# Banded attention with a side network: layer norm shared between GpSimd and VectorE, first transposes row by row, value weights split first, bias additions moved to step 0, output weights of the last pair kept

## Chip, cores and metric

One core of one Trainium2 chip runs the kernel alone. The metric is the device time in microseconds (us), the median over the runs of one kernel. A profile of one further execution goes with it. TensorE (PE) multiplies and transposes, ScalarE (ACT) and VectorE (DVE) work between PSUM and SBUF, GpSimd (POOL) works in SBUF, and all transfers are issued from the queue of SyncE (SP).

## The reference

```
xn  = layernorm(x)                         # x: 8 x 1024 x 512, over the last axis
Q,K,V = xn @ Wq + bq, xn @ Wk + bk, xn @ Wv + bv     # 16 heads of 64
S   = Q K^T where |i-j| <= 64, and 0 elsewhere        # masked scores stay in the softmax as zeros
out = x + (softmax(S) V) @ Wo + bo
        + (sum_h relu(s * W1 + b1) W2 + b2) @ Wout + bout,   s = xn @ Win + bin    # 64 wide, 16 inner
```

All inputs and outputs are float32.

## The kernel before

The batch has 8 items, and the 16 heads are 8 pairs. Every pair of an item is one step, numbered n = 8b + k (b the item, k the pair). There are 64 such steps and two more that drain the pipeline. Step n projects pair k of item b (`proj`), attends to the pair of step n-1 (`attend`) and multiplies the pair of step n-2 with its slice of Wo (`out_proj`). The order of the work on each engine is written out by hand, one function `step` for each engine, and engines wait for each other by counting semaphores. Instructions of one engine start in program order.

Matrix operands are split into a high and a low float32r part, and each product is three passes: high by high, high by low, low by high. The high part is a ScalarE copy, the low part a subtraction: on VectorE where the source is in PSUM, on GpSimd for weights (`split_low`, L328), for the attention output (`output_low`, L364) and for the output weights (L396). A projection (`project`, L1021) is 12 matmuls of 512 columns.

In item 0 (steps 0 to 7) the raw weights of a pair are loaded and split one step ahead, and the split form is also written to DRAM (`w_kept`, `wo_kept`). From item 1 on the split form is loaded from there. The output weights of pair 7 are the exception: `wo_kept` gets pairs 0 to 6 only, and pair 7's are loaded raw and split again in every item, at the end of its k = 0 step (ScalarE L662, then GpSimd L396), and also in step 64 for the last item.

Layer norm: VectorE takes the statistics (L681, L701) and aggregates them (L688). GpSimd then computes four small results: variance plus epsilon (L313), its power -1/2 (L315), mean times that (L318) and the negated shift (L323). ScalarE writes the normalised rows xn (`normalise`, L422), TensorE transposes them (`transpose_x`, L986), ScalarE and VectorE split the transposes (`x_high` L428, `x_low` L695). For item 0 this stands ahead of step 0, in two halves of four row tiles. For item b+1 the statistics are spread over steps k = 3 to 5 of item b, and the four small operations run on GpSimd in step k = 5. There they stand ahead of GpSimd's weight subtractions `split_low(n+1, V)` and `split_low(n+1, Q)` (item 0 only) and of both `output_low`:

```
if attend:
    normalise_weights(1)
if k == 5 and not last:
    layer_norm(b + 1, slice(0, T), b + 3, 4 * b + 8)
if split_next:
    split_low(n + 1, V_)
    split_low(n + 1, Q_)
```

The bias rows bo + bout are added to the accumulator on GpSimd (`add_biases`, L371): four row tiles in step k = 0, two in step k = 1 between the two `normalise_weights`, and two more in step k = 1 between `output_low(0)` and `output_low(1)`.

Other names used below: `mask_scores` (DVE L733, then L739 for the negated row maximum), `exps` (ACT L449), `denominators` (DVE L744, L747, L749), `normalise_weights` (POOL L358), `weigh_values` (PE L1088), `project_out` (PE L1038), `add_output` (DVE L756), `network_out` and `add_network` (PE L1060, DVE L786), `value_lines` (ACT L477).

## Time and profile before

| | us |
|---|---|
| median of 3 runs | 2365.82 (2365.38 to 2368.52) |
| the profiled execution | 2367.19 |
| its span in the trace | 2365.4 |
| PE busy | 2310.1 (98%) |
| DVE busy | 1960.6 (83%) |
| ACT busy | 1576.8 (67%) |
| POOL busy | 892.6 (38%) |

The span is the time from the first to the last instruction in the trace; 1.8 us of the execution lie around it. PE's busy share counts matmuls, whose ends are modelled. The mean granted TensorE clock is 0.996 of 2.4 GHz.

### The profile page before, as it was taken

The numbers are of one execution on the slowest core, as the hardware profiler recorded it, in microseconds if no ns is written. First come the engines' busy times: TensorE is split into PE (matmuls) and PEld (weight loads), VectorE is DVE, ScalarE is ACT, GpSimd is POOL, SyncE is SP. The second block draws the span as 40 slices with busy tenths as digits, with TensorE's granted clock in tenths as the row PEclk, the third lists the DMA queues.
The fourth block names the chain that finished last, engine by engine and source line by source line (L and its number), as shares of the span: only waits on it lengthen the run. The fifth ranks groups of instructions, "written<-read, shape, count | busy, mean of one in ns | idle before, by whom it ended". The sixth has DMA issues, their size and how long they took to land.

```text
span 2365.4 us, 43885 instructions
## 1 busy us (share of the span) xinstructions
PE 2310.1 (98%) x14913; PEld 1975.8 (84%) x14913; DVE 1960.6 (83%) x5088; ACT 1576.8 (67%) x4289; POOL 892.6 (38%) x1302
## 2 busy tenths in 40 slices
PE   5999999999999999999999999999999999999996
PEld 4787888888888888888888888888888888888885
DVE  4887779887898878988889878898879888798886
ACT  3776667666676667666667666766676666676664
POOL 3544435333343324334243332443334332443332
PEclk9999999999999999999999999999999999999999
DMA  4231213221132121421223221331212311122211
GB/s 136 86 125 55 103 59 108 72 72 59 46 123 75 54 75 34 138 65 54 66 63 109 71 57 56 91 98 54 77 46 90 107 55 59 54 89 64 66 47 45
DMA packets 69501, 177.58 MB, mean 75 GB/s; under 512 B 6536, under 2 KB 18848, under 8 KB 69280
## 3 DMA queue, kind: packets, MB, share of 16 engines
q1 hardware_dynamic: 69280, 174.78, 23.6%
q8 instruction: 121, 1.98, 0.3%
q14 instruction: 100, 0.82, 0.1%
HBM read 141.73 MB, written 33.03 MB: 74 GB/s over the span
## 4 chain that ended last, share of the span: by engine, by line
PE 93%; DVE 3%; issue 2%; ACT 1%; POOL 1%; DMA 0%; POOLq 0%; SPq 0%; ACTq 0%; DVEq 0%
PE ps L1021 43%; PE ps L1038 15%; PE ps L1088 12%; PE ps L1076 9%; PE ps L1009 7%; PE ps L1066 2%; PE ps L986 1%; PE ps L1048 1%; DVE probs L733 1%; PE ps L1060 1%; DVE xn L773 1%; DVE v_back L973 0%; ACT probs L449 0%; DVE o_sum L810 0%; DMA acc<-in_L_attn_x 0%
## 5 line engine op out<-in xcount | busy, mean ns | idle before, releaser
L1021 PE MATMUL ps<-xT_hi,w_split 128*128 128x512 f32 x3072 | 1040.7, 400 | 8.1 <-POOL w_split L328 5.0
L358 POOL TENSOR_SCALAR probs<-probs,inv_l,neg_e 128x256 f32<-128x256 f32 x1024 | 569.2, 577 | 638.1 <-DVE neg_e L749 638.1
L1021 PEld LDWEIGHTS ps<-xT_hi,w_split 128*128 128x128 f32 x3072 | 578.4, 188 | 135.3 <-issue 5.2
L449 ACT ACTIVATE probs<-probs,neg_max 128x256 f32<-128x256 f32 x1024 | 507.0, 498 | 142.0 <-DVE neg_max L739 140.9
L1021 PE MATMUL ps<-xT_lo,w_split 128*128 128x512 f32 x1536 | 600.4, 391 | 0.0
L756 DVE TENSOR_TENSOR acc<-ps,acc 128x512 f32<-128x512 f32 x512 | 344.4, 685 | 164.1 <-PE ps L1038 162.6
L500 ACT ACTIVATE pT_hi<-ps 128x512 fp32r<-128x512 f32 x512 | 278.1, 599 | 225.7 <-PE ps L1088 139.5
L364 POOL TENSOR_TENSOR oT_lo<-o_sum,oT_hi 128x512 fp32r<-128x512 f32 x128 | 163.7, 1294 | 682.9 <-ACT oT_hi L516 681.9
L733 DVE CUSTOM_DVE_ANT_0 probs<-ps,mask 128x256 f32<-128x256 f32 x1024 | 372.6, 419 | 31.7 <-PE ps L1009 31.3
L800 DVE TENSOR_TENSOR pT_lo<-ps,pT_hi 128x512 fp32r<-128x512 f32 x512 | 328.2, 684 | 51.1 <-ACT pT_hi L500 50.6
L1038 PE MATMUL ps<-wo_split,oT_hi 128*128 128x512 f32 x1024 | 331.2, 405 | 12.4 <-POOL wo_split L396 5.2
L1021 PEld LDWEIGHTS ps<-xT_lo,w_split 128*128 128x128 f32 x1536 | 290.2, 189 | 51.9
L1088 PE MATMUL ps<-pT_lo,v 128*128 128x256 f32 (+1 forms) x1280 | 306.3, 280 | 0.0
L1088 PE MATMUL ps<-pT_hi,v 128*128 128x256 f32 (+1 forms) x1280 | 302.6, 275 | 0.5 <-DVE pT_lo L800 0.5
L1076 PE MATMUL ps<-ident,probs 128*128 128x128 f32 x2048 | 258.3, 273 | 4.9 <-POOL probs L358 4.0
L1076 PEld LDWEIGHTS ps<-ident,probs 128*128 128x128 f32 x2048 | 230.4, 140 | 23.3 <-issue 3.0
L1088 PEld LDWEIGHTS ps<-pT_lo,v 128*128 128x128 f32 x1280 | 244.1, 191 | 5.1
L1088 PEld LDWEIGHTS ps<-pT_hi,v 128*128 128x128 f32 x1280 | 243.1, 190 | 5.9 <-DVE pT_lo L800 0.8
L1038 PEld LDWEIGHTS ps<-wo_split,oT_hi 128*128 128x128 f32 x1024 | 182.8, 190 | 51.9 <-issue 10.2
L1038 PE MATMUL ps<-wo_split,oT_lo 128*128 128x512 f32 x512 | 201.9, 394 | 0.0
L810 DVE SCALAR_TENSOR_TENSOR o_sum<-ps,v_back,o_part 64x512 f32<-64x512 f32 x256 | 190.8, 745 | 12.9 <-ACT o_part L509 9.0
L449 ACT ACTIVATION_READ_ACCUMULATOR probs<-probs,neg_max 128x1 f32 x1024 | 192.9, 188 | 0.0
(92 smaller groups left out, 3125.1 us busy)
## 6 DMA issues: line engine op xcount, KB each, us to landing
w_split<-w_kept SPq DMA_DIRECT2D x168, 512.0 KB, 3.6
wo_split<-wo_kept SPq DMA_DIRECT2D x49, 512.0 KB, 4.4
out_x<-acc SPq DMA_DIRECT2D x16, 1024.0 KB, 5.9
acc<-in_L_attn_x SPq DMA_DIRECT2D x15, 1024.0 KB, 7.7
w_kept<-w_split SPq DMA_DIRECT2D x24, 512.0 KB, 5.5
wo_raw<-in_L_attn_Wo SPq DMA_DIRECT2D x15, 256.0 KB, 4.8
wo_kept<-wo_split SPq DMA_DIRECT2D x7, 512.0 KB, 3.0
w_raw<-in_L_attn_Wv SPq DMA_DIRECT2D x8, 256.0 KB, 5.5
```

The costliest lines, as they stand in the source:

```text
L358: pool.tensor_scalar(probs[:, h, t], probs[:, h, t], inv_l[:, c:c + 1], neg_e[:, c:c + 1], ALU.mult, ALU.add).then_inc(normed, 1)
L449: act.activation(probs[:, h, t], probs[:, h, t], ACT.Exp, bias=neg_max[:, c:c + 1], accum_out=row_sum[:, c:c + 1])
L500: act.activation(pT[u % 2][hi][:, c * LINE:c * LINE + LINE], ps[PT_BANK[u][c]][:], ACT.Copy) \
L733: dve.tensor_tensor_reduce(out=probs[:, h, t], in0=ps[SCORE_BANK[tp][h]][:, i * WIN:i * WIN + WIN], in1=mask[:], scale=1.0, scalar=0.0, op ...
L756: dve.tensor_tensor(acc[:, parity, t], ps[OUT_BANK[t]][:], acc[:, parity, t], ALU.add) \
L800: dve.tensor_tensor(pT[u % 2][lo][:, cols], ps[PT_BANK[u][c]][:], f32(pT[u % 2][hi][:, cols]), ALU.subtract).then_inc(pT_lo, 1)
L810: dve.scalar_tensor_tensor(o_sum[half][rows], ps[PV_BANK[u]][rows], v_back[rows], o_part[h][rows], ALU.add, ALU.add).then_inc(o_summed, 1)
L1009: last = pe.matmul(ps[SCORE_BANK[tp][h]][:, i * WIN:i * WIN + WIN], qT[qp][rows, t * P:t * P + P], kT[kp][rows, t * P:t * P + WIN], start= ...
L1021: last = pe.matmul(dst[:], w[wp][:, i, c], xT[xp][:, c, half * LINE:half * LINE + LINE], start=(c == 0 and a == 0), stop=(c == KC - 1 and ...
L1038: last = pe.matmul(ps[OUT_BANK[t]][:], oT[op][:, t * P:t * P + P], wo[wp][:], start=(a == 0), stop=(a == 2))
L1076: last = pe.transpose(ps[PT_BANK[u][c]][:, i % 4 * P:i % 4 * P + P], probs[:, h, t, i % 2 * P:i % 2 * P + P], ident[:])
L1088: last = pe.matmul(ps[PV_BANK[u]][:, q0:q0 + (end - first) * P], v[:, (4 * half + c) % T, h].rearrange("p a d -> p (a d)"), pT[h][part][:, ...
```

## The change

- Layer norm. VectorE now adds epsilon right behind the aggregation (`mean_and_variance`), GpSimd keeps the power alone (`inverse_deviation`), and VectorE computes the shift in one instruction (`shift_rows`). In step k = 5 GpSimd's power stands behind the weight subtractions and behind `output_low(0)`, and VectorE's shift is the last instruction of its step.
- Start. x of item 0 is loaded in four quarters, the raw value weights behind the second. ScalarE splits the value weights before it normalises anything, and normalises tiles 0, 1, 4 and 5 only; VectorE writes tiles 2, 3, 6 and 7 (`first_rows`). TensorE transposes tile by tile, 2, 0, 3, 1, each into four PSUM banks, where it had gone bank by bank. VectorE takes the statistics of tiles 4 to 7 between its `x_low`. The value projection of step 0 waits for one `x_low` at a time.
- Bias additions. In item 0 all eight are in step 0.
- Output weights. `wo_kept` also gets pair 7, and from item 1 on the k = 0 step loads it like the others.
- Waits on a value and then on another one of the same semaphore become one wait.

```diff
@@ sync
             def load_output_kept(n, pair):
                 sp.wait_ge(out_done, T * (n - 1))
+                sp.wait_ge(wo_got, 16 * (n - 1))
-            for i in range(2):
+            for i in range(4):
                 sp.dma_start(acc[:, 0, 2 * i:2 * i + 2], x_d[0][:, 2 * i:2 * i + 2]).then_inc(x_quarter[i], 16)
-            load_raw(V_, 0)
-            sp.dma_start(acc[:, 0, 4:T], x_d[0][:, 4:T]).then_inc(x_in[1], 16)
+                if i == 1:
+                    load_raw(V_, 0)
-                if k == PAIRS - 1:
-                    load_output_raw(k, PAIRS - 1 + b)
-                if attend and k > 0:
-                    load_output_kept(n, k - 1)
+                if n == PAIRS:
+                    keep_output(n, PAIRS - 1)
+                elif attend:
+                    load_output_kept(n, (k - 1) % PAIRS)
@@ gpsimd
+            def inverse_deviation(tiles, done):
+                pool.wait_ge(ln_eps, done)
+                pool.tensor_tensor(rstd[:, tiles], var_eps[:, tiles], minus_half[:, tiles], ALU.pow).then_inc(ln_rstd, 1)
-            layer_norm(0, slice(0, 4), 1, 0)
+            inverse_deviation(slice(0, 4), 1)
             split_low(0, V_)
-            layer_norm(0, slice(4, T), 2, 4)
+            pool.memset(mask[:], 1.0).then_inc(pool_set, 1)
+            inverse_deviation(slice(4, T), 2)
             split_low(0, Q_)
             split_low(0, K_)
-                if k == 1 and proj:
+                if k == 1 and proj and b > 0:
                     add_biases(2)
-                if k == 5 and not last:
-                    layer_norm(b + 1, slice(0, T), b + 3, 4 * b + 8)
+                if n == 0:
+                    add_biases(2)
+                    add_biases(3)
                 if attend:
                     output_low(0)
-                if k == 1 and proj:
+                if k == 5 and not last:
+                    inverse_deviation(slice(0, T), b + 3)
+                if k == 1 and proj and b > 0:
                     add_biases(3)
-                if attend and (split or k == 0):
+                if attend and n <= PAIRS:
@@ scalar
-            for t in tiles_of(0):
-                normalise(0, t, small=4 if t == 0 else None)
             split_high(0, V_)
-            for t in tiles_of(1):
-                normalise(0, t, small=8 if t == 4 else None)
+            for t in (0, 1):
+                normalise(0, t)
             for i in range(4):
                 x_high(0, i)
             split_high(0, Q_)
+            for t in (4, 5):
+                normalise(0, t)
             split_high(0, K_)
@@ vector
-            mean_and_variance(tiles_of(0), 4)
-            for t in tiles_of(1):
-                statistics(0, t)
-            mean_and_variance(tiles_of(1), T)
+            mean_and_variance(tiles_of(0), 4, 1)
+            shift_rows(slice(0, 4), 1)
+            first_rows(2)
+            first_rows(3)
             for i in range(4):
+                statistics(0, 4 + i)
                 x_low(0, i)
+            mean_and_variance(tiles_of(1), T, 2)
+            shift_rows(slice(4, T), 2)
+            first_rows(6)
+            first_rows(7)
+                if ln_next and k == 5:
+                    shift_rows(slice(0, T), b + 3)
@@ tensor
-            for i in range(4):
-                if i == 2:
-                    pe.wait_ge(xT_lo, 2)
-                transpose_x(0, i)
+            for t, ready, count in ((2, xn_first, 1), (0, xn_ready, 1), (3, xn_first, 2), (1, xn_ready, 2)):
+                pe.wait_ge(ready, count)
+                for i in range(KC):
+                    last = transpose_tile(0, i, t)
+                    if t == 1:
+                        last.then_inc(xT_done, 1)
@@ tensor, project_out
-                    elif t == 0 and k == 1:
-                        pe.wait_ge(wo_lo, PAIRS - 1 + b)
                     elif t == 0:
-                        pe.wait_ge(wo_got, 16 * (7 * b if k == 0 else 7 * b + k - 1))
+                        pe.wait_ge(wo_got, 16 * (o + 1))
```

`first_rows(t)` waits for the shift and is one `tensor_scalar` of 128x512 with `rstd` and `shift` as its two scalars. `shift_rows` waits for the power and is one `scalar_tensor_tensor` of (mean * -1) * rstd.

## Rows read from the trace of the kernel before

**Rows 1.** Windows: stretch, PE, PEld, DVE, ACT, POOL busy, clock, DMA share, GB/s.
```profile
560.00:840.00 280.00, 279.93 (x1822) 239.93 (x1821) 237.81 (x627) 190.04 (x525) 106.13 (x157) 1.00 0.24 73
```
**Rows 2.** Timeline of PE: start, duration, instruction; in brackets idle before, releaser.
```profile
14.73 1.94 PE L986 MATMUL ps<-ident,xn 128*128 128x128 f32 x8 [14.73 <-ACT xn L422]
...
32.59 0.47 PE L1021 MATMUL ps<-xT_hi,w_split 128*128 128x512 f32 x1
...
77.80 0.63 PE L1076 MATMUL ps<-ident,probs 128*128 128x128 f32 x4 [1.84 <-POOL probs L358]
...
97.92 0.70 PE L1038 MATMUL ps<-wo_split,oT_hi 128*128 128x512 f32 x2 [2.64 <-issue]
...
235.45 0.77 PE L1021 MATMUL ps<-xT_hi,w_split 128*128 128x512 f32 x1 [5.03 <-POOL w_split L328]
...
2349.55 1.19 PE L1038 MATMUL ps<-wo_split,oT_hi 128*128 128x512 f32 x2 [5.17 <-POOL wo_split L396]
```
**Rows 3.** Timeline of all engines ahead of step 0.
```profile
7.67 0.38 DVE L688 BATCH_NORM_AGGREGATE mean_var<-stats 128x2 f32<-128x6 f32 x4
...
8.59 1.05 POOL L315 TENSOR_TENSOR rstd<-var_eps,minus_half 128x4 f32<-128x4 f32 x1
...
10.37 1.28 ACT L422 ACT_TABLE_LOAD   x1 [10.37 <-POOL shift L323]
10.49 2.47 DVE L681 BATCH_NORM_STATS2 stats<-acc 128x6 f32<-128x512 f32 x4 [2.44 <-DMA acc<-in_L_attn_x]
...
11.66 2.93 ACT L422 ACTIVATE xn<-acc,shift,rstd 128x512 f32<-128x512 f32 x4
...
21.47 1.05 ACT L428 ACTIVATE xT_hi<-ps 128x512 fp32r<-128x512 f32 x2
22.07 1.29 DVE L695 TENSOR_TENSOR xT_lo<-ps,xT_hi 128x512 fp32r<-128x512 f32 x2 [8.62 <-ACT xT_hi L428]
```
**Rows 4.** Source views: L197's first load (issued 1.80), L219's 49 loads, L770.
```profile
DMA to landing us min/median/max: 5.6/5.6/5.6
...
DMA to landing us min/median/max: 3.3/4.4/5.9
...
L770 DVE TENSOR_SCALAR xn<-xn,w2c,b2c x8: 540/542/545, 63.0 to 2082.0; 128x512 f32<-128x512 f32 x8
```
**Rows 5.** Timelines of POOL and DVE in steps 0 and 1.
```profile
51.08 5.48 POOL L371 TENSOR_TENSOR acc<-acc,bias_row 128x512 f32<-128x512 f32 x4
...
71.76 2.74 DVE L744 SCALAR_TENSOR_TENSOR row_l<-e,row_sum 128x8 f32<-128x8 f32 x1 [1.11 <-ACT e L452]
...
71.93 2.54 POOL L371 TENSOR_TENSOR acc<-acc,bias_row 128x512 f32<-128x512 f32 x2
...
92.39 2.99 POOL L371 TENSOR_TENSOR acc<-acc,bias_row 128x512 f32<-128x512 f32 x2
```
**Rows 6.** Chain that ended last, merged pieces: start, duration, work.
```profile
99.03 2.86 PE ps L1009 x24
...
235.45 4.40 PE ps L1021 x12
...
524.98 2.75 PE ps L1021 x12
...
533.69 1.62 PE ps L1009 x24
```
**Rows 7.** Timelines of POOL, ACT and DVE, item 1, steps k = 5 and 6.
```profile
525.51 1.96 POOL L315 TENSOR_TENSOR rstd<-var_eps,minus_half 128x8 f32<-128x8 f32 x1
...
526.32 0.62 ACT L516 ACTIVATE oT_hi<-o_sum 128x512 fp32r<-128x512 f32 x1
...
528.68 1.29 DVE L786 TENSOR_TENSOR acc<-ps,acc 128x512 f32<-128x512 f32 x2 [0.56 <-PE ps L1060]
...
531.37 0.17 DVE L739 TENSOR_SCALAR neg_max<-row_max 128x4 f32<-128x4 f32 x1
```
**Rows 8.** Timeline of POOL in step 64.
```profile
2345.74 2.49 POOL L364 TENSOR_TENSOR oT_lo<-o_sum,oT_hi 128x512 fp32r<-128x512 f32 x2 [7.36 <-ACT oT_hi L516]
```

More of the change, by code:

```diff
@@ L171, in tiles_of, with xT_bank, wait_for_rows @@
             return range(4 * half, 4 * half + 4)
-        def first_steps(n):
-            return n if isinstance(n, int) else 2
+        def xT_bank(b, i):
+            return FIRST_XT_BANK[i] if b == 0 and i < KC else XT_BANK[i]
+        def wait_for_rows(engine, b, half):
+            if b == 0:
+                engine.wait_ge(xn_ready, 2 * half + 2)
+                engine.wait_ge(xn_first, 2 * half + 2)
+            else:
+                engine.wait_ge(xn_ready, T * b + 4 * half)
         def run_steps(engine, step):
@@ L295, in _ @@
                 sp.wait_ge(stored[half], 16 * B)
-            sp.wait_ge(x_in[0], 16 * (B - 1))
-            sp.wait_ge(x_in[1], 16 * B)
+            for half in range(2):
+                sp.wait_ge(x_in[half], 16 * (B - 1))
         @block.gpsimd
@@ L652, in step @@
                 if ln_next and k == 5:
[L653 removed]
+                    normalise(b + 1, 0)
                 if attend:
                     output_high(1)
[L656 to L658 removed]
+                if attend and n <= PAIRS:
+                    act.wait_ge(wo_in, 16 * (j + 1))
+                    if T * j > 0:
                         act.wait_ge(out_done, T * j)
[L660 removed]
+                    if j > 0:
                         act.wait_ge(wo_got, 16 * j)
@@ L689, in mean_and_variance, with shift_rows, first_rows @@
                 last.then_inc(ln_agg, 1)
+                cols = slice(tiles[0], tiles[-1] + 1)
+                dve.wait_ge(ln_agg, done)
+                dve.tensor_scalar(var_eps[:, cols], mean_var[:, cols, 1], EPS, None, ALU.add).then_inc(ln_eps, 1)
+            def shift_rows(cols, done):
+                dve.wait_ge(ln_rstd, done)
+                dve.scalar_tensor_tensor(shift[:, cols], mean_var[:, cols, 0], -1.0, rstd[:, cols],
+                                         ALU.mult, ALU.mult).then_inc(ln_shift, 1)
+            def first_rows(t):
+                dve.wait_ge(ln_shift, 1 + t // 4)
+                dve.tensor_scalar(xn[:, t], acc[:, 0, t], rstd[:, t:t + 1], shift[:, t:t + 1], ALU.mult, ALU.add) \
+                    .then_inc(xn_first, 1)
             def x_low(b, i):
@@ L760, in network_line @@
                     rows = slice(half * M, half * M + M)
-                    if half == 0 and isinstance(b, int) and b == 0:
+                    if half == 0 and b == 0:
                         dve.wait_ge(const_in, 16 * N_CONST)
@@ L807, in output_sum @@
                     dve.wait_ge(v_back_ready, j + 1)
-                    if h == 0 and begun(2 * j - 1 + half):
+                    if h == 0 and 2 * j - 1 + half > 0:
                         dve.wait_ge(oT_lo, 2 * j - 1 + half)
@@ L1019, in project @@
                     for c in range(KC):
+                        if n == 0 and i == V_ and half == 0:
+                            pe.wait_ge(xT_lo, c + 1)
                         for a, (wp, xp) in enumerate(PASSES):
@@ L1042, in network_in @@
                 def network_in(half):
-                    if half == 0 and isinstance(b, int) and b == 0:
+                    if half == 0 and b == 0:
                         pe.wait_ge(win_ready, 1)
```

146 lines of the change are left out of this document (53 added, 93 removed).

## The prediction

> **What bounds the kernel now.** I read the windows first, then TensorE's timeline for its idle times, then the timelines of the other engines around each of these, and the chain. In the stretch from 560 to 840 us TensorE is busy for 279.93 of 280 [rows 1]: from item 1 to item 7 nothing but TensorE's own work sets the time, and the change leaves that work alone. So it can win only where TensorE is idle, and lose where it makes TensorE wait. The idle times are few [rows 2]: the start (TensorE's first work is at 14.73, and the first query projection of step 0, from where it is busy for a long stretch, starts at 32.59), 1.84 ahead of 77.80, 2.64 ahead of 97.92, 5.03 ahead of 235.45, and 5.17 ahead of 2349.55. The span is 2365.4 against 2310.1 busy, so 55 us in all.
>
> An idle time costs more than itself. After the 5.03 the 12 matmuls of a projection took 4.40, where they take 2.75 in the steady part; after the 2.64 the 24 score matmuls took 2.86 against 1.62 [rows 6]. That is the lower level of the clock, 1.2 against 2.4 GHz, with a rate of 0.43 against 0.23 per matmul. After the 1.84 the next rows are at the full rate.
>
> **Start.** All times from here are my schedule of the new program, built from durations of rows. The aggregation ends at 8.05 [rows 3]. VectorE adds epsilon, the power (1.05) runs from 8.35 to 9.4. The value weights are issued third as before, at 1.80, and land after 5.6 [rows 4], at 7.4. ScalarE's table load (1.28), which stood on the path from 10.37, now runs from 7.4 to 8.7, hidden behind the power; the high copy (0.6) ends at 9.3. So GpSimd goes from the power straight into the value weights' subtraction, 1.27 (two passes of that shape take 2.54 [rows 5]), until 10.7. VectorE's shift wants to start at 9.5. Here the trace speaks against the change: at 71.76 VectorE's `row_l`, 8 columns wide with both inputs in SBUF, took 2.74, and ended with the two GpSimd additions that ran from 71.93 to 74.47 [rows 5]. I take the same here: the shift is held until 10.7, and VectorE's first row tile comes right after it.
>
> The Trainium skill (SBUF — State Buffer, Who interferes with whom) says that VectorE and GpSimd share a port pair under an exclusive lock, and that a VectorE instruction with two SBUF inputs or in a two-port mode fully waits for a GpSimd instruction that started first. By this rule, the trace agrees, and `shift_rows` and `first_rows` are both of the kinds that wait. Without the rule the start would gain 7.7, with it 4 (both are worked out here from rows).
>
> The row tiles: VectorE's take 0.54 [rows 4], ScalarE's 2.93 for four, so 0.73 each [rows 3]. TensorE starts at 11.6 with tile 2, and 16 transposes at the rate of 8 in 1.94 [rows 2] end at 15.5. The high copies follow at 0.53 each; VectorE's chain of four low parts (1.29 for two) with three statistics in between (2.47 for four) [rows 3] runs from 15.6 to 20.2. The value projection goes along with it and is done by 21.9. Then aggregation, epsilon and power end at 22.1. The query weights' subtraction starts on GpSimd at once and holds the shift again, to 23.4. ScalarE's tiles 4 and 5 end at 25.1, the key weights' copy and the value lines (0.6 and 0.8) at 26.4, the sixth set of transposes at 27.4. So the first query projection starts at 27.4 and not at 32.59: 5.2 less. But TensorE has been idle from 21.9 to 25.1, longer than the 2.64 that lost the clock, and that projection will run at the low level, for up to 1.65 more (4.40 less 2.75). I take a gain of 4.0; bounds 2 (both holds and one more) and 7.7 (no hold of 1.3 and 1.2, no clock lost). The four statistics that were one block and SP's one more issue (about 0.5, ahead of the query weights, which are needed at 17) are hidden.
>
> **Steps 0 and 1.** The four bias additions that join step 0 are 5.1 to 5.5 of GpSimd [rows 5], from 56.6 to about 62. Behind them on GpSimd stands the low part of the key weights of step 1, which moves from 57.3 to 62 to 63; TensorE wants it at 64.2. Not on the path, with 1 to spare. What VectorE does meanwhile with two SBUF inputs (the cast and subtraction of the network's output weights, the two negations of row maxima) is held by up to 1.27 each, three or four times, and the exponentials of step 1 hang on it. In return the two additions leave the middle of step 1, and `row_l` takes 0.2 and not 2.74. TensorE's 1.84 ahead of 77.80 stands behind that chain. Together: 2.6 recovered, about 3 to 3.5 lost. I take 1.0 lost; bounds 1.8 gained (the idle time goes) and 4 lost.
>
> **Step 1 to 2.** The 2.64 ahead of 97.92 is the wait for pair 0's output weights (L396). GpSimd's queue there is `output_low(0)`, two additions (92.39 to 95.38 [rows 5]), `output_low(1)`, L396. With the additions gone L396 ends at 94.9, before TensorE gets there at 95.28. Removed: 2.64, plus 1.24 of the slow scores, plus about 0.4 for the projections beside them. What is late next is VectorE's masks of step 2, which TensorE reaches earlier: about 0.6 of waits. Gain 3.5; bounds 2.6 and 4.4.
>
> **Step 5 to 6 of item 0.** The 5.03 ahead of 235.45 is the wait for the value weights' low part, behind GpSimd's layer norm. Now that stands first, and is done ten us early. Removed: 5.03 + 1.65. Next in GpSimd's queue are `output_low(0)`, the power (1.96 [rows 7]), `output_low(1)`, L396; ScalarE's `normalise` waits for the shift and stands ahead of its second `oT_hi`, on which the last two wait. I get L396's end at 239.9, and TensorE there at 238.5, after its projection, network output, scores and second projection: a wait of 1.5, short enough to keep the clock (rows at 77.80). Gain 5.2; bounds 3 and 6.7.
>
> **The same place in items 1 to 6.** There is no idle time to win there. VectorE's shift waits for the power, and the power for `output_low(0)`: `oT_hi` ends at 526.94 [rows 7], 1.3 and 1.96 later the power is done at 530.3. The instruction behind the shift, `add_network`, started at 528.68 and now starts at 530.6; the masks behind it, done at 531.3, are done at 533.2. TensorE wants them at 533.69 [rows 6]. The second masks and the first `add_output` have about 0.4 to spare as well; ScalarE's value lines have 0.2. I take nothing lost; bounds 0 and 0.5 in each of six items, 3 in all. Two small operations less on GpSimd, and ScalarE's and GpSimd's split of pair 7's weights, gone from six items, lie beside TensorE's work: nothing.
>
> **Tail.** TensorE waits to 2349.55 for pair 7's low part, behind both `output_low`. The load of the kept weights can start when the last product with pair 6's is done. Between that and the idle time (from 2344.38) lie the ten matmuls of `weigh_values(3)`, 1.1, so it starts at 2343.4. It lands after 3.3 to 5.9, median 4.4 [rows 4]: at 2347.8. The first `output_low` is done by 2347.0 (half of 2.49 behind 2345.74 [rows 8]). Gain 1.8; bounds 0.3 and 2.5. The clock falls all the same. In items 1 to 7 the load has some 9 us until its use.
>
> **Sum.** 4.0 - 1.0 + 3.5 + 5.2 + 0 + 1.8 = 13.5 less, so 2353.7 for an execution like the profiled one of 2367.19 (span 2365.4 plus 1.8). The median is 1.4 below that one: 2352.3.
>
> **Rivals.** First, VectorE isn't held: it issues before GpSimd, or the held pieces are off the path. Then the start gives 7.7, step 1 gains 1.0, and the next two places give 4.2 and 5.7: 20.4, so 2345.4. For it: the shift and the subtraction want to start within 0.1 of each other, and who is first is open. Chance 0.2.
>
> Second, the bias additions hold VectorE in step 1 to the full, 4 lost, and the wait behind it is long enough to lose the clock, 1.6 more: 13.5 - 3 - 1.6 = 8.9, so 2356.9. For it: the 2.74 of `row_l`, in which VectorE was let in between no two additions. Against: the one-column sums of step 0 got in after one. Chance 0.12.
>
> Third, other waits take most of the place of the two that go at 97.92 and 235.45, since VectorE and ScalarE run as late as before: half of 8.7 lost, 2356.7. Against: these engines are idle there too. Chance 0.08.
>
> Fourth, the other side: VectorE's wait for the power comes through to TensorE in every item. Its place is the boundary of k = 5 and 6. From 528.2 to 530.6 it is 2.4; if TensorE loses all of that and the clock with it, 4.05 in six items is 24.3, so 2376.6. It decides against the change from 2.25 lost per item. Against: the 0.4 to 0.5 to spare above. Chance 0.03.
>
> **Numbers.** The forecast has 0.57. Its own range is 2349 to 2356. With the first three rivals the range is 2345 to 2359. About 0.2% (4.7 us) is what a measurement of this kernel can tell from no change. Only the worst of every bound, 0.9 less in all, or the fourth rival end above 2361: faster 0.92, same 0.05, slower 0.03.
>
> **What would show it.** The first query projection near 27.4 and slow; VectorE's first shift long, or ended with GpSimd's subtraction; the second score set of step 2 at 1.62 in 24 matmuls; no wait of V weights in step 6, and one of 1 to 2 for L396's product; in items 1 to 6 TensorE still without idle time and `add_network` two us later; the last `project_out` 1 to 2.5 earlier. I am wrong if TensorE shows idle time after 560, if the start moves by less than 2, or if step 1 costs over 4.

## The result, and the profile after

The changed kernel takes 2344.3 us (median of four executions, 2343.91 to 2348.97) against 2366.38 before (four, on the same chip): a ratio of 0.991, with a 95% interval of 0.989 to 0.992. It is 22.1 us faster. The forecast was 2352.3, 13.5 less, with a range of 2345 to 2359, so the time lies 0.7 below the range.

The profiled execution took 2344.28 with a span of 2342.6, so 22.9 less than the one that the forecast's sum was made against. TensorE issues 14913 matmuls in both. Numbered in order, they show where the changed kernel gets ahead, and by how much:

| place | forecast | gain in the profile |
|---|---|---|
| start, to the end of the first query projection | 4.0 | 5.9 |
| steps 0 and 1 | -1.0 | 1.0 |
| step 1 to 2 | 3.5 | 3.7 |
| step 5 to 6 of item 0 | 5.2 | 5.3 |
| step 8 (first of item 1) | 0 | 0.8 |
| items 1 to 7, up to the tail | 0 | 0.3 |
| tail | 1.8 | 6.0 |

The steady part, windows as in [rows 1], shows no idle time, as before:

```profile
540.00:820.00 280.00, 279.94 (x1818) 239.66 (x1816) 236.59 (x626) 189.45 (x524) 103.23 (x153) 1.00 0.24 75
```

The timeline of the start, all engines (answers to [rows 2] and [rows 3]):

```profile
0.78 1.28 ACT L382 ACT_TABLE_LOAD   x1 [0.78 <-PEq L1337]
...
6.70 0.63 ACT L382 ACTIVATE w_split<-w_raw 128x512 fp32r<-128x512 f32 x1 [4.64 <-DMA w_raw<-in_L_attn_Wv]
...
9.05 1.22 DVE L658 SCALAR_TENSOR_TENSOR shift<-mean_var,rstd 128x4 f32<-128x4 f32 x1 [1.22 <-POOL rstd L294]
...
10.31 1.00 DVE L663 TENSOR_SCALAR xn<-acc,rstd,shift 128x512 f32<-128x512 f32 x2
11.00 3.65 PE L962 MATMUL ps<-ident,xn 128*128 128x128 f32 x16 [11.00 <-DVE xn L663]
...
20.56 1.22 DVE L658 SCALAR_TENSOR_TENSOR shift<-mean_var,rstd 128x4 f32<-128x4 f32 x1 [1.13 <-POOL rstd L294]
...
23.43 2.16 PE L962 MATMUL ps<-ident,xn 128*128 128x128 f32 x8 [3.30 <-ACT xn L388]
...
25.24 0.78 PE L1004 MATMUL ps<-xT_hi,w_split 128*128 128x512 f32 x1
```

The shift is held twice for 1.22, as forecast. The query projection starts at 25.24 where the forecast had 27.4.

The timeline of TensorE in steps 0 to 6 of item 0, the rows with the idle times that answer to the four middle ones of [rows 2]:

```profile
48.22 1.09 PE L1047 MATMUL ps<-ident,vT 128*128 128x128 f32 x8 [1.11 <-DVE vT L797]
...
64.76 1.06 PE L1057 MATMUL ps<-ident,probs 128*128 128x128 f32 x8 [0.84 <-POOL probs L326]
...
66.90 1.06 PE L1057 MATMUL ps<-ident,probs 128*128 128x128 f32 x8 [1.08 <-POOL probs L326]
...
70.90 0.66 PE L1057 MATMUL ps<-ident,probs 128*128 128x128 f32 x4 [0.18 <-DVE pT_lo L776]
...
88.57 0.71 PE L1019 MATMUL ps<-wo_split,oT_hi 128*128 128x512 f32 x2 [0.19 <-issue]
...
229.03 0.71 PE L1019 MATMUL ps<-wo_split,oT_hi 128*128 128x512 f32 x2 [1.18 <-issue]
```

The 1.84 is 0.18 now, the 2.64 is 0.19, and the 5.03 is gone; in its place 1.18 stands ahead of pair 4's product, where the forecast had 1.5. New is the 0.84. The 1.08 was there before too, as 1.09, and so was the 1.11, ahead of the value transposes, as TensorE's timeline of the kernel before shows:

```profile
54.23 1.09 PE L1066 MATMUL ps<-ident,vT 128*128 128x128 f32 x8 [1.08 <-DVE vT L821]
```

Last the tail, in the timeline and in the windows:

```profile
2328.76 2.50 POOL L332 TENSOR_TENSOR oT_lo<-o_sum,oT_hi 128x512 fp32r<-128x512 f32 x2 [7.35 <-ACT oT_hi L480]
...
2330.16 0.70 PE L1019 MATMUL ps<-wo_split,oT_hi 128*128 128x512 f32 x2 [2.77 <-POOL oT_lo L332]
...
2333.57 4.10 DVE L732 TENSOR_TENSOR acc<-ps,acc 128x512 f32<-128x512 f32 x6 [1.05 <-PE ps L1019]
```

```profile
2329.00:2338.00 9.00, 6.00 (x24) 4.35 (x24) 5.49 (x8) 0.57 (x1) 2.26 (x2) 1.00 0.24 91
```

The idle time is 2.77 and not 5.17, and the granted clock of the eight products is 1.00; in the same nine microseconds before, 2349 to 2358, it was 0.50, and TensorE got 17 matmuls done where it now does 24. A pair of matmuls takes 0.70, not the 1.19 of [rows 2]. The six additions of VectorE stand without a gap: VectorE, not TensorE, sets the end.

The changed kernel's profile does lose the clock once in the tail, 18.6 us earlier. TensorE had stopped four times, for 0.97, 0.71, 0.37 and at last 1.95 us (to 2311.60), and then:

```profile
2311.84:2315.26 3.42, 3.42 (x9) 2.60 (x9) 3.16 (x13) 3.05 (x14) 3.02 (x6) 0.50 0.00 0
```

This cost almost nothing (the lead is 16.8 us before it and 16.9 behind it), since TensorE waits for other engines there. The kernel before has the same four stops at this place, the last of 1.99, and kept the clock.

### The profile page after: what moved, and what is told of

Read it like the earlier page. It is cut to its first block, busy times and chain, and to the rows that moved or that the text cites. A ratio compares the mean times of both kernels' runs of the same rounds, so it can differ in the third digit from the quotient of the medians.

```text
span 2342.6 us, 43340 instructions
## 1 busy us (share of the span) xinstructions
PE 2306.1 (98%) x14913; PEld 1972.7 (84%) x14913; DVE 1957.9 (84%) x5110; ACT 1566.9 (67%) x4278; POOL 871.1 (37%) x1268
## 4 chain that ended last, share of the span: by engine, by line
PE 93%; DVE 4%; ACT 1%; issue 1%; POOL 0%; DMA 0%; SPq 0%; ACTq 0%; POOLq 0%
PE ps L1004 43%; PE ps L1019 15%; PE ps L1069 12%; PE ps L1057 9%; PE ps L990 7%; PE ps L1047 2%; PE ps L962 1%; PE ps L1029 1%; PE ps L1041 1%; DVE probs L709 1%; DVE xn L749 1%; DVE v_back L949 0%; DVE neg_max L715 0%; ACT probs L415 0%; DVE acc L732 0%
```

## The experiments

They were measured in three rounds, each with its own executions of the kernel before. Its medians are 2367.18 (kept weights alone and undone, bias additions alone, layer norm alone), 2366.96 (start alone, low parts behind the rows, additions moved and cut) and 2367.21 (the last three). The ratios are against these, so medians of different rounds compare to about 1 us.

### The kept output weights of pair 7 alone

The kernel before, with only the part of the diff that keeps pair 7.

```diff
-                if k == PAIRS - 1:
-                    load_output_raw(k, PAIRS - 1 + b)
-                if attend and k > 0:
-                    load_output_kept(n, k - 1)
+                if n == PAIRS:
+                    keep_output(n, PAIRS - 1)
+                elif attend:
+                    load_output_kept(n, (k - 1) % PAIRS)
```

> The kernel before with the output weights of pair 7 kept, and nothing else. Theory A, the shorter idle time in the tail also keeps TensorE's clock: idle ahead of the last products 2.8 and not 5.17, the 24 products at 0.23 and not 0.43 each, 6.0 to 6.3 us less in all, and the same in nearly every execution. Theory B, the clock in the tail is a matter of where the program stands, not of this idle time: 2.4 less, with the products still at 0.43, or 6 less in some executions and 2.4 in others. In items 1 to 7 no difference by either.

Measured: 2360.2 (nine executions, 2359.4 to 2365.24), ratio 0.9975 (0.9966 to 0.9985). The profiled execution took 2360.2. Its gain is 0.1 up to step 7, 0.9 after step 8, 1.0 at the start of the tail and 7.0 at its end. TensorE's timeline and the window around it:

```profile
2346.11 0.70 PE L1037 MATMUL ps<-wo_split,oT_hi 128*128 128x512 f32 x2 [2.77 <-POOL oT_lo L365]
```

```profile
2345.00:2354.00 9.00, 5.99 (x24) 4.35 (x24) 5.47 (x8) 0.51 (x1) 2.21 (x2) 1.00 0.25 93
```

So this part alone brings 7.0 in an execution that keeps the clock (without step 8, 6.2, where theory A had 6.0 to 6.3): 0.8 in step 8, 2.4 of idle time, 3.3 by rate in the first sixteen of the last matmuls, and 0.3 behind. The nine executions fall into two groups, five from 2359.4 to 2360.2 at a mean clock of 0.998 and four from 2363.85 to 2365.24 at 0.995, with nothing between. Only the profiled one has a trace; that the others lost the clock in the tail is read from their mean clock. By that reading it is the second form of theory B, 6 less in some executions and 2.4 in others.

### The changed kernel without the kept weights of pair 7

The same part undone in the changed kernel.

> The changed kernel with pair 7's output weights split again in every item, as before. Theory A: idle of 5.2 in the tail, clock lost, 6.0 to 6.3 us more than the changed kernel, so about 2350.5. Theory B: 2.4 more, about 2346.7, with the clock kept in the tail.

Measured: 2351.54 (five executions, 2350.23 to 2351.78), ratio 0.993 (0.992 to 0.994), 7.2 above the changed kernel, or 6.4 when each is taken against the kernel before of its own round. Between the two profiles it is 7.0. TensorE's timeline and a window over the same nine microseconds:

```profile
2333.51 1.20 PE L1020 MATMUL ps<-wo_split,oT_hi 128*128 128x512 f32 x2 [5.17 <-POOL wo_split L366]
```

```profile
2333.00:2342.00 9.00, 7.71 (x17) 5.65 (x18) 3.33 (x5) 0.00 (x0) 0.40 (x1) 0.50 0.02 8
```

The idle time is 5.17 again, the clock falls, and the 0.8 of step 8 are lost. By the profiles the part is worth 7, undone or done alone.

### The bias additions alone

```diff
-                if k == 1 and proj:
+                if k == 1 and proj and b > 0:
                     add_biases(2)
...
+                if n == 0:
+                    add_biases(2)
+                    add_biases(3)
```

and the same condition ahead of `add_biases(3)` in step 1, in the kernel before.

> The kernel before with all eight bias additions of item 0 in step 0, nothing else. By the two traces: the wait of 2.64 ahead of 97.92 goes, with its 1.6 at the low clock, 0.6 of other waits come (3.65), and steps 0 and 1 gain 1.0: 4.6 less. By the prediction's term for steps 0 and 1: 1.0 lost there, 2.6 less in all. If the idle time of 2.64 was all that counts, 2.6 + 1.0.

Measured: 2362.54 (ten executions, 2361.22 to 2363.54), ratio 0.998 (0.997 to 0.999). By place in the profile: 0.9 in steps 0 and 1 (from the end of the first query projection), 3.7 at step 1 to 2, 0.8 given back in step 6, and 2.3 in the tail, where the clock was back at 1.00 from 2349.1 in this execution. Steps 0 and 1 gain, where the forecast had a loss. The wait ahead of the value transposes is 1.08 as before, and for the 1.84 stands one of 0.87, at the first weight transposes of the step:

```profile
71.34 1.06 PE L1079 MATMUL ps<-ident,probs 128*128 128x128 f32 x8 [0.87 <-POOL probs L358]
```

The 0.8 of step 6 is the clock. The wait there is 5.02, as before, but the clock stayed at 0.50 from 229.4 to 236.3, so for nearly all of the projection behind it; in the kernel before it was back 3.0 us into that projection. The chain has 5.23 for what took 4.40 [rows 6]:

```profile
231.42 5.23 PE ps L1024 x12
```

### Item 0's additions cut to one column

In the changed kernel each of item 0's eight bias additions adds one column and not 512; the output of item 0 lacks the bias in the other 511.

```diff
+                        cols = slice(0, 1 if b == 0 else E)
-                        pool.tensor_tensor(acc[:, b % 2, t], acc[:, b % 2, t], bias_row[:], ALU.add) \
+                        pool.tensor_tensor(acc[:, b % 2, t, cols], acc[:, b % 2, t, cols], bias_row[:, cols], ALU.add) \
                             .then_inc(bias_added, 1)
```

> The changed kernel with item 0's eight bias additions cut to one column each, so item 0's output lacks the bias in the other columns: what the additions cost in steps 0 and 1. Theory A, they hold VectorE: the idle times of steps 0 and 1 (1.6, 1.1, 0.84, 1.08) shrink by 2 us or more in sum. The prediction's rival, that they cost 4: 4 us less. Theory B, they are hidden: under 0.5 us.

Measured: 2344.82 (four, 2342.79 to 2345.18). Steps 0 and 1 gain 3.2 and not 1.0, kept up to the last product; the tail gives it back, and 0.7 more, in the profiled execution, whose last products ran slower: the clock was at 0.50 from 2329.0 to 2335.9. VectorE's timeline in the changed kernel:

```profile
45.17 1.22 DVE L793 TENSOR_TENSOR v_mean<-v_mean,v_sums 128x1 f32<-128x1 f32 x1
...
46.62 1.54 DVE L797 TENSOR_SCALAR vT<-vT,v_new 128x1024 f32<-128x1024 f32 x1
...
55.27 1.02 DVE L715 TENSOR_SCALAR neg_max<-row_max 128x4 f32<-128x4 f32 x1
```

and with one column:

```profile
45.27 0.16 DVE L794 TENSOR_TENSOR v_mean<-v_mean,v_sums 128x1 f32<-128x1 f32 x1
...
45.65 0.75 DVE L798 TENSOR_SCALAR vT<-vT,v_new 128x1024 f32<-128x1024 f32 x1
...
53.98 0.17 DVE L716 TENSOR_SCALAR neg_max<-row_max 128x4 f32<-128x4 f32 x1
```

Three operations are held by 1.06, 0.79 and 0.85, and a fourth, the low part of the network's output weights (`wout_lo`), by 0.97. The wait of 1.11 ahead of the value transposes and the 0.84 ahead of the weight transposes are gone. So all eight additions cost 2.2 in these two steps: 1.3 in step 0 and 0.9 in step 1.

The 1.3 isn't the price of the change. Four additions stood in step 0 before, and there the first two of the operations took 1.22 and 1.55 as well, with the 1.08 ahead of the value transposes. What the four moved additions cost is the 0.9: they reach `wout_lo` (0.69 before, 1.66 now) and `neg_max` (0.17 before, 1.02 now).

### The additions behind the centred values

The changed kernel, with GpSimd waiting for `v_centered` ahead of item 0's additions, and the key weights' low part moved between `add_biases(1)` and `add_biases(2)`.

```diff
+                if n == 0:
+                    pool.wait_ge(v_centered, 1)
                 if k == 0 and proj:
                     add_biases(0)
                     add_biases(1)
                 if n == 0:
+                    split_low(1, K_)
                     add_biases(2)
```

> The changed kernel, but in step 0 GpSimd's bias additions wait for VectorE's centred values, and the key weights' low part stands between the first four and the last four. Theory A, VectorE is held in the middle of step 0 by the additions: its two one-column sums take 0.2 each and not 1.2, the centring 0.8 and not 1.55, TensorE's wait of 1.1 ahead of the value transposes goes, and step 1 starts about 1 us earlier; the last four additions then run in step 1 and hold VectorE's small operations there, which costs part or all of it: between 1 us less and 1 us more. Theory B, they are slow by themselves: same durations, and 0 to 1 us more.

Measured: 2347.46 (four, 2347.01 to 2348.94), ratio 0.992 (0.990 to 0.993). TensorE's timeline:

```profile
59.92 0.50 PE L1007 MATMUL ps<-xT_hi,w_split 128*128 128x512 f32 x1 [0.41 <-DVE row_max L712]
...
64.90 1.06 PE L1060 MATMUL ps<-ident,probs 128*128 128x128 f32 x8 [1.96 <-POOL probs L326]
```

and VectorE's:

```profile
54.54 1.01 DVE L718 TENSOR_SCALAR neg_max<-row_max 128x4 f32<-128x4 f32 x1
...
56.95 1.09 DVE L718 TENSOR_SCALAR neg_max<-row_max 128x4 f32<-128x4 f32 x1
```

The wait ahead of the value transposes is gone, as meant. But the additions that came later now hold two `neg_max` and not one, and what was 0.84 is 1.96, with 0.41 new. Steps 0 and 1 gain 0.5 less than in the changed kernel: the hold was moved, not removed. The rest of the 3 us lies in the tail, whose last products ran slower in this profile: the clock was at 0.50 from 2331.3, 0.9 behind the idle time of 2.77, to 2338.1.

### The layer norm behind the weight subtractions alone

```diff
-                if k == 5 and not last:
-                    layer_norm(b + 1, slice(0, T), b + 3, 4 * b + 8)
                 if split_next:
                     split_low(n + 1, V_)
                     split_low(n + 1, Q_)
+                if k == 5 and not last:
+                    layer_norm(b + 1, slice(0, T), b + 3, 4 * b + 8)
```

In the kernel before; the four small operations stay on GpSimd, ahead of both `output_low`.

> The kernel before with GpSimd's four layer norm operations of step k = 5 moved behind the two weight subtractions, nothing else. Theory A, the wait ahead of 235.45 is only GpSimd's order: the 5.03 and the 1.65 of the slow projection go, a wait of about 1.8 for the output weights' low part comes in step 6 (four operations stand before both output_low, not one): 4.9 less. Theory B, much of the gain in this place came from the shift on VectorE and the power behind output_low(0): 3 or less, with a wait of over 3 in step 6. No change in items 1 to 7 by either.

Measured: 2362.17 (nine, 2359.4 to 2362.61), ratio 0.9975 (0.9965 to 0.9984). By place: 2.1 behind the kernel before by 103 us, since its start was 0.6 slower and the clock was at 0.50 from 79.8 to 83.2 in this execution, which cost 1.6, then 6.65 ahead of that at step 5 to 6, and nothing from there to the end. Items 1 to 6 don't move (4.51 at 320 us, 4.60 at the tail). The stop ahead of that low clock is the same as the one of 1.84 in the kernel before, which kept the clock:

```profile
78.33 0.63 PE L1076 MATMUL ps<-ident,probs 128*128 128x128 f32 x4 [1.85 <-POOL probs L358]
```

```profile
79.80:83.20 3.40, 3.40 (x18) 3.40 (x18) 1.70 (x4) 0.60 (x1) 2.21 (x2) 0.50 0.00 0
```

GpSimd's timeline and the chain of waits show how little stands between:

```profile
238.95 1.30 POOL L396 TENSOR_TENSOR wo_split<-wo_raw,wo_split 128x512 fp32r<-128x512 f32 x1
```

```profile
240.56 0.72 PE ps L1038 x3
```

The subtraction ends at 240.25, 0.3 ahead of TensorE: the wait of 1.8 that theory A had for step 6 didn't come. Its total of 4.9 less is met by the median (5.0), but by luck, as at its place the part brings 6.65. So the wait of 5.03 with the slow projection behind it is worth 6.7, the sum that the forecast had as "removed"; the changed kernel keeps 5.3 of it, because there the same product waits 1.18. The changed kernel has the power behind `output_low(0)` and the shift on VectorE. That this order costs the 1.4 is argued from the two profiles; the two kernels differ in other parts too.

### The start alone

The changed kernel without the kept weights of pair 7, with the bias additions in step 1 again and the power ahead of the weight subtractions:

```diff
-                if k == 1 and proj and b > 0:
+                if k == 1 and proj:
                     add_biases(2)
...
+                if k == 5 and not last:
+                    inverse_deviation(slice(0, T), b + 3)
                 if split_next:
                     split_low(n + 1, V_)
```

> The changed kernel with the other parts undone: bias additions of item 0 back in steps 0 and 1, the power of step k = 5 ahead of the weight subtractions, pair 7's output weights split again in every item. What is left is the new start and the layer norm shared with VectorE. By the two traces: 5.9 less than the kernel before, at the first query projections; the waits ahead of L396's product in step 2 (2.6) and of the value projection in step 6 (about 5) and the 5.2 in the tail are back. By the prediction: 4.0 less. If the parts depend on each other, the sum of the four parts alone misses the 22 of the whole by more than 3.

Measured: 2357.15 (five, 2356.78 to 2361.06), ratio 0.996 (0.995 to 0.998). The start gains 6.7 in its profile and 7.0 by 103 us. The gap between this and the changed kernel's 5.9 is where the clock's low stretch lies: 23.2 to 26.6 here, 21.5 to 28.3 there, over the same projection. The old idle times are back: 1.84, 2.63 and 5.17 as they were, and 3.99 in place of 5.03, since GpSimd's part of the layer norm is now the power alone. This brings 0.9 more in step 6. The last 2.4 of the profile's 10.4 lie in the tail, where behind the same 5.17 the clock was back after 3.4 us (at 2344.3), and not after 10.2 as in the kernel before.

By the medians the four parts alone bring 9.8, 4.6, 5.0 and 7.0, together 26.4, and the whole 22.1. They miss it by 4.3, over the 3 that was set as the sign that the parts depend on each other. They do, as far as the profiles show: the 0.9 here is part of the same wait that the layer norm's place removes, that place is worth 1.4 less beside the rest, and what the clock gives back in the tail counts in three of the four.

### The low parts of the weights behind the normalised rows

The changed kernel, with two waits on GpSimd, so that VectorE's shift and row tiles come first:

```diff
             inverse_deviation(slice(0, 4), 1)
+            pool.wait_ge(xn_first, 2)
             split_low(0, V_)
             pool.memset(mask[:], 1.0).then_inc(pool_set, 1)
             inverse_deviation(slice(4, T), 2)
+            pool.wait_ge(xn_first, 4)
             split_low(0, Q_)
```

> The changed kernel, but ahead of step 0 GpSimd starts the value weights' subtraction after VectorE's row tiles 2 and 3, and the query weights' after tiles 6 and 7. Theory A, the 1.22 that each shift_rows takes is a wait for GpSimd's subtraction: both take 0.2, TensorE's first transpose comes 1.1 earlier, the second shift 2.2 earlier, 2 us less in all, unless the value projection then waits for its low weights. Theory B, a shift of four columns with two inputs takes 1.2 by itself on this engine: it stays 1.2, the subtractions only come later, and the kernel is 0 to 2 us slower.

Measured: 2344.84 (four: 2342.17, 2343.37, 2346.3, 2346.54), ratio 0.990 (0.989 to 0.992). The timeline of the start:

```profile
9.31 0.16 DVE L660 SCALAR_TENSOR_TENSOR shift<-mean_var,rstd 128x4 f32<-128x4 f32 x1 [1.22 <-POOL rstd L294]
9.51 1.52 ACT L390 ACTIVATE xn<-acc,shift,rstd 128x512 f32<-128x512 f32 x2 [1.92 <-DVE shift L660]
...
10.21 3.44 PE L964 MATMUL ps<-ident,xn 128*128 128x128 f32 x16 [10.21 <-DVE xn L665]
...
19.77 0.16 DVE L660 SCALAR_TENSOR_TENSOR shift<-mean_var,rstd 128x4 f32<-128x4 f32 x1 [1.13 <-POOL rstd L294]
...
21.05 2.70 POOL L298 TENSOR_TENSOR w_split<-w_raw,w_split 128x512 fp32r<-128x512 f32 x2 [1.31 <-DVE xn L665]
21.20 1.40 DVE L691 TENSOR_TENSOR win<-win_raw,win 128x256 fp32r<-128x256 f32 x1
```

The shift takes 0.16, not 1.22, twice, as theory A had it. The start gains 8.0 and not 5.9, and the 2.0 stay up to the last products. The hold moves to the network's weights (1.40, where it took 0.43 in the changed kernel), and nothing waits for those. But this execution lost the clock in the tail, behind the same idle time as the changed kernel's:

```profile
2328.19 1.19 PE L1021 MATMUL ps<-wo_split,oT_hi 128*128 128x512 f32 x2 [2.77 <-POOL oT_lo L334]
```

### The changed kernel again, and two with a shorter stop in the tail

The first is the changed kernel unchanged. In the second, pair 7's kept weights are loaded for step 65 into the value weights' buffer, as soon as the last value projection is done, and products 0 and 4 of step 65 wait for `oT_hi` first and for `oT_lo` only ahead of their third matmul. The third has this and the two waits of the experiment before.

```diff
@@ sync
-                sp.wait_ge(out_done, T * (n - 1))
+                sp.wait_ge(v_proj if n == B * PAIRS else out_done, 2 * n if n == B * PAIRS else T * (n - 1))
                 sp.wait_ge(wo_got, 16 * (n - 1))
-                sp.dma_start(f32(wo_split[:]), wo_kept[pair]).then_inc(wo_got, 16)
+                dst = w_split[:, V_].rearrange("p a c q -> p a (c q)") if n == B * PAIRS else wo_split[:]
+                sp.dma_start(f32(dst), wo_kept[pair]).then_inc(wo_got, 16)
@@ tensor, project_out (final: the last pair of the last item)
                     if t % 4 == 0:
-                        pe.wait_ge(oT_lo, 2 * o + t // 4 + 1)
+                        pe.wait_ge(oT_hi if final else oT_lo, 2 * o + t // 4 + 1)
                     for a, (op, wp) in enumerate(PASSES):
+                        if final and t % 4 == 0 and a == 2:
+                            pe.wait_ge(oT_lo, 2 * o + t // 4 + 1)
```

> The changed kernel once more, for the spread of its executions. Theory A: the 2.8 us idle ahead of the last eight products costs the clock in some executions and not in others, as it did with the kept weights alone (four executions of nine near 2364.5, five near 2359.8). Then the times fall into two groups, near 2344.2 at a mean clock of 0.997 to 0.999 and 3.5 to 4.7 above at 0.995, with nothing between. Rival B: the one time of 2348.97 was an outlier of another kind; then all lie within 1 us of 2344.3.

Measured: 2345.21 (four: 2344.03, 2344.14, 2346.28, 2349.0), ratio 0.991 (0.989 to 0.993). With the first four that makes five executions of eight from 2343.9 to 2344.3, and three above: 2346.28, 2348.97 and 2349.0. Two groups, but with one time between them. The median of all eight is 2344.3.

> The changed kernel, but the last load of the kept output weights (pair 7, step 64) goes into the buffer of the value weights, which is free by then, as soon as the last value projection is done, and the first two matmuls of products 0 and 4 of step 65 wait for the high part of the attention output alone. TensorE's idle time ahead of the last products should fall from 2.8 to about 1.4 (oT_hi at 2328.7 where oT_lo is at 2330.0), with a second stop of about 0.6 ahead of the third matmul. Theory A: VectorE's first addition comes 0.7 earlier and the clock is kept in every execution: 2343.6, all executions within 1 us. Rival B, the clock at the end doesn't depend on this idle time: some executions in five still near 2348. Rival C, the load and not the low part released TensorE: then the gain is over 1.5.

Measured: 2344.3 (four: 2343.01, 2344.26, 2344.35, 2348.49), ratio 0.990 (0.989 to 0.992). TensorE's timeline:

```profile
2329.39 0.70 PE L1024 MATMUL ps<-w_split,oT_hi 128*128 128x512 f32 x2 [1.42 <-ACT oT_hi L481]
...
2330.67 0.51 PE L1024 MATMUL ps<-w_split,oT_lo 128*128 128x512 f32 x1 [0.58 <-POOL oT_lo L333]
```

The idle times are those expected, 1.42 and 0.58, and the first product comes 1.35 earlier against the rest of its profile. By the sixteenth matmul 0.5 of that is left, since VectorE's additions set the pace. Its start was 0.5 slower than that of the changed kernel's profile, so the profiled time is the same. And one execution of four took 2348.49. So the times didn't lie within 1 us as theory A had it; a stop of 1.4 didn't end the slower executions. No trace shows where this one lost its 4 us.

> The changed kernel with both edits: GpSimd takes the low part of the value and query weights of the start behind VectorE's normalised rows (2.0 us earlier up to the tail, as measured), and the last load and first products as in the tail experiment. Theory A: the gains add, 2.0 and 0.7, and no execution loses the clock at the end: 2341.5, all within 1 us. Rival B: the clock at the end falls in some executions all the same, then the median is 2342 to 2345 with a spread of 4.

Measured: 2341.53 (four: 2340.91, 2341.51, 2341.55, 2344.1), ratio 0.989 (0.9875 to 0.990). Its profile is 2.3 ahead of the changed kernel's at the end of the start and 2.75 at the end of the last product; the window of the tail has the full clock. The gains add, as expected; that all executions lie within 1 us didn't come true, the fourth is 2.6 above the others. It is the fastest version of this study, 2.8 below the changed kernel; its interval overlaps the changed kernel's, and three of its four executions lie below every one of the changed kernel's.

```profile
2326.00:2335.00 9.00, 6.29 (x24) 4.27 (x24) 6.13 (x9) 1.04 (x2) 2.52 (x2) 1.00 0.21 79
```

## Why the prediction was wrong, point by point

**The step that failed** is in the tail: "The clock falls all the same." It had the shorter stop right (1.8 forecast, 2.4 measured, bound 2.5) and the clock wrong: behind 2.77 of idle time it stayed full in the profiles of the changed kernel (twice) and of the kept weights alone. That is 3.6 more, and the tail brought 6.0. With 6.0 here the forecast would have been 2348.1, inside its range. Of the 9.4 us that the profile gained over the sum, 4.2 are from here, 2.0 from steps 0 and 1, 1.9 from the start, 0.8 from step 8 and the rest from small differences. The prediction had in the 2.64 of [rows 2] an idle time of the same size that lost the clock [rows 6], and took one case for the rule. Three other profiles show the same 2.77 with the clock lost: the experiment with the GpSimd waits for 10.2 us, the two with the additions moved and cut for 6.8 each. So neither "it falls" nor "it stays" holds for such a stop: it is three of six profiles each way, and the price belongs in the range as a coin toss. The two outcomes have traces only in different kernels. That both happen with one and the same kernel is read from times and mean clocks: the changed kernel's 2348.97 and 2349.0 have 0.995, where its profiles have 0.997 and 0.998. With the GpSimd waits, where the clock was lost, the tail brought 2.0, close to the forecast; that the median escaped the range is in part luck.

Nor is a shorter stop safe, as the prediction took from the 1.84 ahead of 77.80 ("short enough to keep the clock"). In four profiles with that stop the clock fell once, behind 1.85 in the layer norm's experiment, at a cost of 1.6 us. And the four stops 17 to 21 us ahead of the last products, the last of them 1.94 to 2.00, stand in all thirteen profiles; the clock fell there in eight of them. What decides isn't settled here.

**What released TensorE there** was not the load, as the step had it. Issued at 2326.31 and 3.3 in flight, it was there at 2329.6; GpSimd's first `output_low` ended at 2330.0. The load was 1.1 faster than the median taken.

**Start** (4.0 forecast, 5.9 measured) was mis-sized. Both holds came as forecast: the shift starts 0.06 behind GpSimd's subtraction and takes 1.22. Without them the start gains 2.1 more. The slow query projection came too, and the value projection ahead of it ran at the full rate. What was off is the schedule between them. The quarters of x brought the aggregation to 7.63 and not 8.05, so TensorE started at 11.0 and not at 11.6. VectorE's chain of four low parts and three statistics began 0.9 earlier than planned and took 4.3 and not 4.6, to 18.9. And ScalarE's next two row tiles, directly behind the shift, ended at 23.3 and not at 25.1. The first query projection came 2.2 earlier than planned. The table load ran at 0.78 where the schedule had it at 7.4; it was off the path in the plan too. The slow projection in the chain, 4.11 where the forecast had 4.40:

```profile
25.59 4.11 PE ps L1004 x12
```

The start is the same in six kernels and gains between 5.4 and 6.7 in their seven profiles. They differ in the clock: in three of them the value projection ran at the low level as well, until 19.2 to 20.5.

**Steps 0 and 1** (-1.0 forecast, 1.0 measured) had the wrong sign. The term added up what VectorE gets back (2.6) and loses (3 to 3.5), and not what of it reaches TensorE. `row_l` fell from 2.74 to 0.20 as said, but TensorE's wait behind it was 1.84, of which 1.7 went. The moved additions held two more operations of VectorE, by 0.97 and 0.85, and TensorE saw 0.84. The other two holds, with the wait ahead of the value transposes, were there before. The bias additions alone show the same: 1.84 gone, 0.87 new, 0.9 gained.

The first two rivals fell. The number of the first, 2345.4, is nearest to the result, but its mechanism is shown wrong by the rows: VectorE was held at both shifts and four times beside the additions, and TensorE waited for it. The second had 4 lost and the clock with it; 0.9 were, and the clock held in the changed kernel.

**Step 1 to 2** (3.5 forecast, 3.7 measured) was right, in place and mechanism: 0.19 of wait, the second set of scores at 1.63 for 24. **Step 5 to 6** (5.2 forecast, 5.3 measured) was too: the V weights' wait gone, 1.18 ahead of pair 4's product at the full clock, 6.7 without that wait. The third rival, other waits for half of these two gains, had one wait right and its size wrong.
**Step 8** (0 forecast, 0.8 measured) the prediction had missed. Its list of idle times left out this row of the kernel before:

```profile
319.98 0.70 PE L1038 MATMUL ps<-wo_split,oT_hi 128*128 128x512 f32 x2 [0.64 <-issue]
```

It is the first product with pair 6's output weights. At k = 0 the kernel before waits there for `wo_got` at 7b, in item 1 the landing of the seventh copy to `wo_kept`, which SyncE issued at 317.01, and not for the split that it needs. The changed kernel waits for `wo_lo` at this place. The idle time is gone in all eight profiles with pair 7 kept, and 0.59 to 0.64 in the five without.

**Items 1 to 6** (0 forecast, 0.3 measured) was right, and the fourth rival, a stall in each item, with it wrong. VectorE's timeline in item 1, to be held against [rows 7]:

```profile
513.23 0.17 DVE L658 SCALAR_TENSOR_TENSOR shift<-mean_var,rstd 128x8 f32<-128x8 f32 x1 [1.59 <-POOL rstd L294]
513.31 1.28 DVE L762 TENSOR_TENSOR acc<-ps,acc 128x512 f32<-128x512 f32 x2
...
516.00 0.17 DVE L715 TENSOR_SCALAR neg_max<-row_max 128x4 f32<-128x4 f32 x1
```

and the chain:

```profile
513.33 2.94 PE ps L1004 x12
516.27 0.68 PE ps L1019 x3
516.95 1.62 PE ps L990 x24
```

VectorE does wait 1.59 for the power. Its masks are done at 516.0, and TensorE takes them at 516.95: 0.95 to spare where 0.5 was forecast.

**What the parts bring.** Alone against the kernel before: the start 6.7 to 7, the bias additions 4.6 up to step 2, the layer norm's place 6.7 (5.3 beside the rest), the kept weights 7.4 by the median of the group that kept the clock and 2.5 by that of the other. All four work at the ends of the program and in item 0; the 2015 us from 320 us to the tail changed by 0.3.

## What to carry to other kernels

A stop of TensorE has two prices, its length and what the clock does behind it. Here the second came behind some stops of 1.85 to 2.77 us and not behind others, in the same place of the program, so it goes into a range as two cases with a chance each; one trace of each kernel can't tell, the list of all executions can. And when a small VectorE operation and a GpSimd operation are released by the same event, say which goes first, and then follow the hold to TensorE, since only the part that makes TensorE wait counts: two waits of GpSimd for the rows that VectorE writes behind its small operation were worth 2 us in the start, while the same idea in step 0 only moved the hold to the next small operation.

## What the runs showed of the hardware

- Behind the same idle time of 2.77 us, at the same place of nearly the same programs, TensorE went on at the full granted clock in three profiles (0.70 for two matmuls of 512 columns) and lost it in three, at once (1.19) or within 0.9 us. Behind 5.17 it was lost in all five, for 3.4 us in two and 10.2 in three; behind 2.62 to 2.64, in step 2, in all four; behind 1.84 or 1.85 in one of four. Of nine executions of the kept weights alone five were near 2359.8 and four near 2364.7. Between the changed kernel and the one with GpSimd's waits, half the clock cost 3.3 over the first sixteen matmuls and 4.0 to the end.
- Transposes alone raised the clock: TensorE's first work in the changed kernel is 16 of them, at 11.0 to 14.65, and the granted clock is 1.00 from 14.67 on, with the value projection at the full rate (0.47 and 0.40 a matmul). In four of the nine profiles with the new start it rose only at 18.9 to 20.5, and the first matmul of the projection took 0.76 or 0.77. Eight transposes took 1.94 at the start of the kernel before and 1.06 where the clock was 1.00.
- ScalarE's table load stood ahead of the first activation's wait: 0.78 when that activation waited for a DMA, against 10.37 [rows 3] when the function's first activation waited for GpSimd. It took 1.28, on the path before and off it after. No run here tells which difference moved it.
- A four-column VectorE operation that started 0.06 behind a GpSimd subtraction of 512 columns took 1.22, and 0.16 when GpSimd came behind it. `row_l` of [rows 5] began before the two additions, 0.2 ahead of the end of GpSimd's last weights, and ended with the second of them, so it didn't get in between. `neg_max`, 4 columns with one SBUF input, took 1.02 beside the additions against 0.17, and one of 1024 columns 1.54 against 0.75. The Trainium skill (SBUF — State Buffer, Who interferes with whom) says that a VectorE instruction of these kinds waits in full for a GpSimd instruction that started first; by this rule, the traces agree for the shift, `neg_max` and the 1024 columns.
